# Denominators' reciprocals taken on 128 partitions by way of transfers, and a new order of visits in an attention loop

## The chip, the cores and the metric

The kernel runs on one core of one Trainium2 chip. The metric is the device time of one execution in microseconds (us); the lower the better. Three timed executions of the kernel before took 1839.34, 1840.99 and 1845.72 us, so the median is 1840.99 us.

## The reference

The program computes two residual layers, `x = x + s * g`, each with layer norm. Layer 0 has softmax attention with 16 heads of 64 over 4 batches of 1024 tokens, with 128 features (`s`), and a gated mixture of 8 experts with top-2 routing (`g`). Layer 1 has a linear recurrence and a block-quantised feed-forward. The change touches only the attention of layer 0:

```
q, k, v = split(X @ W_qkv)                      # 16 heads of 64
scores  = q . k / sqrt(64)
weights = softmax(scores)
attn    = weights @ v
s       = attn.reshape(b, s, 16 * 64) @ W_out
```

## The kernel before

`layer0_attention` handles heads two at a time: there are N = 4 batches x 8 = 32 **pairs**. A pair has two halves of 512 queries (`hf` 0 and 1) and in each half 8 key tiles of 128 (KT), so 16 **steps** t. In a step TensorE (PE) makes the scores of 128 keys by 512 queries for two heads (`scores`, six matmuls into `ps_s`), ScalarE (ACT) takes exp into `probs`, GpSimd (POOL) adds the tile to `psum_k` (the sums over keys), and PE multiplies a tile by V (`values`, into `ps_v`). The softmax needs each query's maximum beforehand: PE makes the products again in single precision rounding (`max_products`, into `ps_three`) and VectorE (DVE) reduces them (`row_max`, L1581, or the split forms L1591, L1596, L1603). The maxima of a half are ready in the middle of the half before; `spread` (L1175, L1177) sends them to DRAM and reads them back to 128 partitions (`peak`), and ACT, or DVE for the steps in `BY_V`, writes them negated into `ps_s` before the scores (`seed`).

Two steps make a **visit** (VISITS = 8). Each visit has room for other PE work, the items of the list `VISIT`: the projections of the pair to come (`K0`, `K1`, `Q0`, `Q1`), its V rows (`V0`, `V1`), the denominators (`den1`, `den0`: a matmul of `psum_k` with ones, copied to `den` by ACT, L1453) and the output projection of the pair before (`out0`, `out1`, added to `sT` by DVE, `add_out`, L1641). All of them go through one bank, `ps_x`. That bank is also the last of the three banks of `ps_three`: a visit whose item is not a K or Q projection is **SHARED**, and its second maximum uses banks 1 and 2 (`ps_mx`), so that PE need not wait for DVE to read all of the first maximum. In a visit with a projection both maxima use banks 0 and 1 (`ps_m`), and the second waits until the first is read (`m_done`).

The order of each engine is written out by hand. Before, the visits are K1; Q0 with den1; out0; V0; Q1 with den0; out1; V1; K0: the SHARED visits stand in pairs (out0 and V0, out1 and V1), and of the projections K0, K1 and Q0 follow one another. The reciprocals of the denominators are four DVE instructions of 128x128 a half (`inverse`, L1622), placed between maxima; `normalise` (L1635) multiplies `raw` (the values that ACT took out of `ps_v`) by them; out0 or out1 waits for it.

SyncE (SP) issues all of the direct transfers in one row of instructions. In each pass of its loop, which covers an even and an odd pair, it waits for the last values of the pair before (`v_ready`), then issues `move(1)` (V, 512 KB), `xs_hi` and `xs_lo` (512 KB each), and then the `spread` of each half, with the expert weights' parts between. At the end of the pass it waits for the V1 copy of the odd pair and issues `move(0)`. After the loop, SP waits for that move, and loads the first rows and weights of the next stage.

Of the kernel before, what the change touches and what calls it, by code (L numbers as in the profile page):

```python
# [14 lines left out]
P = 128  # L15
# [967 lines left out]
def layer0_attention(nc, ctx, g):  # L983
# [10 lines left out]
    PARTS = 4  # L994
# [3 lines left out]
    LATE_PRESETS = 5  # L998
# [13 lines left out]
    warm = sb("warm", [P, 1], F32)  # L1012
    x_rows = sb("x_rows", [P, 2, ROW], F32)
# [47 lines left out]
    rden_done = sem("rden_done")  # L1061
# [11 lines left out]
    ones_n_done = sem("ones_n_done")  # L1073
# [5 lines left out]
    VISIT = [("K1",), ("Q0", "den1"), ("out0",), ("V0",), ("Q1", "den0"), ("out1",), ("V1",), ("K0",)]  # L1079
# [4 lines left out]
    BY_V = (3, 13)  # L1084
# [58 lines left out]

    def chunk(name):
        return slice(int(name[1]) * CH, (int(name[1]) + 1) * CH)
# [7 lines left out]
    with nc.Block() as block:  # L1153
        @block.sync
        def _(sp):
# [24 lines left out]
            spread(0, 0)  # L1180
            sp.wait_ge(xa_done, AHEAD["a"])
            move(0)
            with sp.Fori(0, N // 2) as i:
# [6 lines left out]
                spread(n * 2 + 1, 1)  # L1190
                expert_part(n)
                load_part(n + 1)
                spread(n * 2 + 2, 0)
                spread(n * 2 + 3, 1)
                expert_part(n + 1)
                load_part((n + 2) % N)
                spread(n * 2 + 4, 0)
                sp.wait_ge(xa_done, reads(n + 1, "V1"))
                move(0)
            sp.wait_ge(peak_in, (N * 2 + 1) * 16)  # L1200
            sp.wait_ge(we_in, (N + 1) * 16)
# [13 lines left out]
        def _(pe):  # L1215
            def bank_free(n, name):
                names = FIRST if n is None else LAST if n is N else LIST
                at = names.index(name)
                if n is None:
                    if at >= 2:  # L1220
                        pe.wait_ge(READ[READER[names[at - 2]]], reads(n, names[at - 2]))
                elif at:
                    before = names[at - 1]
                    pe.wait_ge(READ[READER[before]], reads(n, before))
                else:
                    pe.wait_ge(xv_done, n * PER["v"] + AHEAD["v"])
# [132 lines left out]
            pe.wait_ge(ones_n_done, 1)  # L1359
# [23 lines left out]
            for n, par in pairs(pe):  # L1383
                for t in range(STEPS):
                    p = t // 2
                    b = (n + (2 if p == VISITS - 1 else 1)) // PAIRS % B
# [41 lines left out]
        def _(act):  # L1428
# [9 lines left out]
            def read(n, name, par):  # L1438
# [12 lines left out]
                else:  # L1451
                    act.wait_ge(rden_done, n * 2 + (2 if name == "den0" else 1))
# [38 lines left out]
            for n, par in pairs(act):  # L1491
                for t in range(STEPS):
# [9 lines left out]
                    if p not in SHARED:  # L1502
                        read(n, VISIT[p][0], par if p == VISITS - 1 else 1 - par)
# [14 lines left out]
                    if p == 5:  # L1518
# [7 lines left out]
        def _(pool):  # L1526
            nc.gpsimd.memset(ones_n[:, :], 1.0).then_inc(ones_n_done, 1)
# [22 lines left out]
            for n, par in pairs(pool):  # L1550
                for t in range(STEPS):
# [14 lines left out]
                    if t != STEPS - 5:  # L1566
# [8 lines left out]
        def _(v):  # L1575
# [55 lines left out]
            def normalise(n, hf):  # L1631
                k = n * 2 + (1 if hf else 2)
                v.wait_ge(rden_done, k + 1)
# [27 lines left out]
            def tiles_of_experts():  # L1661

                v.wait_ge(n_ready, 2)
                v.wait_ge(ones_n_done, 1)
# [48 lines left out]
            v.sem_inc(rden_done, 1)  # L1713
# [27 lines left out]
            for n, par in pairs(v):  # L1741
# [6 lines left out]
                step(0)  # L1748
                step(1)
                low(n, "K1", nxt)  # L1750
                seed(n, 3)
                step(2)
                step(3)
                low(n, "Q0", nxt)
                expert_part(n)
                row_max_upper(n, 4)
                row_max_lower(n, 4)
                inverse(n, 1, 0)
                row_max_shared(n, 5)
                inverse(n, 1, 1)  # L1760
                row_max_upper(n, 6)
                add_out(n, "out0")
                row_max_lower(n, 6)
                row_max_shared(n, 7)
                inverse(n, 1, 2)
                step(8)
                inverse(n, 1, 3)
                step(9)
                low(n, "Q1", nxt)
                normalise(n, 1)  # L1770
                row_max_upper(n, 10)
                row_max_lower(n, 10)
                inverse(n, 0, 0)
                row_max_shared(n, 11)
                seed(n, 13)
                row_max_upper(n, 12)
                add_out(n, "out1")
                row_max_lower(n, 12)
                inverse(n, 0, 1)
                row_max_shared(n, 13)  # L1780
                inverse(n, 0, 2)
                step(14)
                inverse(n, 0, 3)
                step(15)
                low(n, "K0", par)
                normalise(n, 0)
# [675 lines left out]
def program(nc, args, out):  # L2462
# [6 lines left out]
    g.peaks = nc.dram_tensor("peaks", (2, 2 * CH), F32, kind="Internal").ap()  # L2469
    g.results = nc.dram_tensor("results", (2 * NT + ROUTED * CH, D), F32, kind="Internal").ap()  # L2470
# [88 lines left out]
```

## Time and profile before

| What | Value |
|---|---|
| Median of three executions | 1840.99 us |
| The profiled execution's own time | 1841.47 us |
| Its span | 1839.6 us |
| PE busy | 1727.4 us (94%) |
| DVE busy | 1547.9 us (84%) |
| ACT busy | 1459.2 us (79%) |
| POOL busy | 1444.4 us (79%) |
| TensorE's granted clock, mean | 0.98 of full speed |

The span is the time between the first and the last instruction of the profiled execution. Busy times are sums over instructions; a busy PE is not a PE at its peak, since matmuls overlap and their ends are modelled. The attention loop takes from about 75 to 1421 us of the span: 16 passes of two pairs.

### The profile page before, as it was taken

The page shows a single profiled execution, that of the slowest core. Times are in us where ns is not written, and L with a number is a line of the kernel's source. Part 1 is how long each engine was busy: PE and PEld are TensorE (multiplying, and loading weights), DVE is VectorE, ACT ScalarE, POOL GpSimd, SP SyncE. Part 2 cuts the span into 40 slices and gives each one's busy share as a digit, 9 for nine tenths or more (in the row PEclk, how much of TensorE's full clock was granted, in tenths as well). Part 3 has the DMA queues.
Part 4 walks back from the last instruction along what each step waited for, and adds up shares of the span by engine and source line. Part 5 has one row for each costly group of instructions (what it writes and reads, how often), then busy time and mean ns, then how long its engine had stood idle before and what let it go on. Part 6 is the DMA issues. An engine that isn't in the chain of part 4 may idle for free. (4 is left out here: it accounts for less than half of the span.)

```text
span 1839.6 us, 32373 instructions
## 1 busy us (share of the span) xinstructions
PE 1727.4 (94%) x9247; PEld 924.8 (50%) x9247; DVE 1547.9 (84%) x2180; ACT 1459.2 (79%) x1954; POOL 1444.4 (79%) x869
## 2 busy tenths in 40 slices
PE   5899999999999999999999999999999899975687
PEld 5444444444444444444444444444444677763456
DVE  7888888888888888888888888888888878888886
ACT  4488888888888888888888888888888777864553
POOL 5388888888888888888888888888888256654664
PEclk9899999999999999999999999999999999997899
DMA  7212121212212121212122121212122777331000
GB/s 258 79 36 80 36 80 46 80 46 69 78 52 86 34 80 36 80 46 80 46 69 82 51 83 34 80 36 80 46 80 62 241 218 218 115 99 48 0 18 29
DMA packets 125334, 143.31 MB, mean 78 GB/s; under 512 B 26737, under 2 KB 106673, under 8 KB 122098
## 3 DMA queue, kind: packets, MB, share of 16 engines
q1 hardware_dynamic: 120306, 132.61, 23.6%
q0 software_dynamic: 4992, 10.27, 1.7%
q8 instruction: 16, 0.26, 0.1%
q14 instruction: 20, 0.16, 0.0%
HBM read 87.20 MB, written 27.64 MB: 62 GB/s over the span
## 5 line engine op out<-in xcount | busy, mean ns | idle before, releaser
L1562 POOL TENSOR_TENSOR psum_k<-psum_k,probs 128x1024 f32<-128x1024 f32 x384 | 929.3, 2420 | 103.9 <-ACT probs L1499 83.8
L1499 ACT ACTIVATE probs<-ps_s 128x1024 f32<-128x1024 f32 x512 | 497.0, 1024 | 149.9 <-PE ps_s L1319 149.9
L1328 PE MATMUL ps_v<-probs,V 128*64 128x512 f32 x2056 | 497.8, 605 | 0.0
L1581 DVE TENSOR_REDUCE mxh<-ps_three 128x2 f32<-128x1024 f32 x264 | 318.5, 1207 | 98.3 <-PE ps_three L1286 98.2
L1483 ACT ACTIVATE ps_s<-peak 128x1024 f32<-128x1024 f32 x224 | 245.1, 1132 | 0.0
L1483 ACT ACTIVATE ps_s<-qkv_raw 128x1024 f32<-128x1024 f32 x224 | 245.0, 1131 | 0.0
L1622 DVE RECIPROCAL e_y_row<-e_y_row 128x128 f32<-128x128 f32 x256 | 241.0, 941 | 0.0
L1328 PEld LDWEIGHTS ps_v<-probs,V 128*64 128x64 f32 x2056 | 124.8, 136 | 228.6 <-issue 209.7
L1319 PE MATMUL ps_s<-e_ew 64*128 64x512 f32 x1536 | 199.0, 391 | 0.0
L1562 POOL TENSOR_TENSOR psum_k<-probs 128x1024 f32<-128x1024 f32 x64 | 152.8, 2388 | 47.2 <-ACT probs L1499 39.4
L854 POOL DMA_INDIRECT results<-e_y_row,e_y_at x92 | 102.6, 1115 | 82.0 <-ACT e_y_row L795 52.8
L1319 PEld LDWEIGHTS ps_s<-e_ew 64*128 64x128 f32 x1536 | 144.6, 185 | 28.6 <-ACT ps_s L1483 2.7
L1603 DVE TENSOR_REDUCE mxh<-ps_three 128x2 f32<-128x1024 f32 x128 | 150.7, 1178 | 0.1
L1591 DVE TENSOR_REDUCE mxh<-ps_three 128x1 f32<-128x512 f32 x128 | 88.5, 692 | 72.3 <-PE ps_three L1286 70.7
L1286 PE MATMUL ps_three<-e_ew 64*128 64x512 f32 x528 | 131.8, 495 | 6.3 <-DVE mxh L1581 4.9
L1286 PE MATMUL ps_three<-k_hi,q_hi 64*128 64x512 f32 x512 | 126.6, 490 | 0.8
L1286 PEld LDWEIGHTS ps_three<-e_ew 64*128 64x128 f32 x528 | 52.2, 193 | 134.5 <-issue 80.9
L1286 PEld LDWEIGHTS ps_three<-k_hi,q_hi 64*128 64x128 f32 x512 | 50.2, 191 | 125.0 <-issue 79.5
L1319 PE MATMUL ps_s<-q_hi,k_hi 64*128 64x512 f32 x512 | 101.3, 391 | 0.0
L1319 PE MATMUL ps_s<-q_lo,k_hi 64*128 64x512 f32 x512 | 101.2, 390 | 0.0
L1319 PE MATMUL ps_s<-q_hi,k_lo 64*128 64x512 f32 x512 | 100.9, 389 | 0.0
L779 ACT ACTIVATE e_relu<-e_ps_z 128x512 f32<-128x512 f32 x124 | 74.6, 602 | 33.0 <-PE e_ps_z L708 30.0
(320 smaller groups left out, 3184.4 us busy)
## 6 DMA issues: line engine op xcount, KB each, us to landing
e_ew<-w_split SPq DMA_DIRECT2D x23, 1024.0 KB
qkv_raw<-peaks SPq DMA_DIRECT2D x33, 512.0 KB, 3.9
V<-e_x_raw SPq DMA_DIRECT2D x33, 512.0 KB, 3.6
peak<-peaks SPq DMA_DIRECT2D x32, 512.0 KB, 4.3
xs_hi<-xh SPq DMA_DIRECT2D x16, 512.0 KB, 4.0
xs_lo<-xl SPq DMA_DIRECT2D x16, 512.0 KB, 5.0
rows<-in_blank_d SPq DMA_DIRECT2D x4, 1483.5 KB, 16.9
e_x_raw<-rows SPq DMA_DIRECT2D x23, 258.0 KB
```

Source lines behind the costliest of these rows:

```text
L779: nc.scalar.activation(r[:, q % NZ, :], ps_z[q % NZ][:, :], ACT.Relu).then_inc(relu_done, 1)
L854: nc.gpsimd.indirect_dma_start(g.results[:, :], bass.IndirectOffsetOnAxis(ap=y_at[s][:, t, 0:1], axis=0), y_row[s][:, t, :], None).then_in ...
L1286: ins = nc.tensor.matmul(m[:, x, :], q[rows, :], k_hi[par][rows, kh * CH:(kh + 1) * CH], start=True, stop=True)
L1319: ins = nc.tensor.matmul(o[:, x, :], lhs[par][rows, keys], rhs[par][rows, qs], start=False, stop=True, skip_group_check=True)
L1328: ins = nc.tensor.matmul(ps_v[rows, :], V[par][:, kt, rows], probs[:, t % RING, x, :], start=kt == 0, stop=kt == KT - 1)
L1483: nc.scalar.activation(ps_s[t % 2][:, :, :], peak[hf][:, :, :].rearrange("p c x -> p x c"), ACT.Copy, scale=-1.0).then_inc(seeded, 1)
L1499: nc.scalar.activation(probs[:, t % RING, :, :], ps_s[t % 2][:, :, :], ACT.Exp, scale=SCALE).then_inc(p_done, 1)
L1562: nc.gpsimd.tensor_tensor(acc, probs[:, (t - 1) % RING, :, :] if kt == 1 else acc, probs[:, t % RING, :, :], ALU.add).then_inc(add_done, 1)
L1581: nc.vector.tensor_reduce(mxh[:, kh, t, :], max_bank(unit, i)[:, :, :], AX.X, ALU.max).then_inc(m_done, 1)
L1591: nc.vector.tensor_reduce(mxh[:, kh, q, 1:2], ps_m[:, 1, :], AX.X, ALU.max).then_inc(m_upper, 1)
L1603: nc.vector.tensor_reduce(mxh[:, kh, q, :], ps_mx[:, :, :], AX.X, ALU.max).then_inc(m_done, 1)
L1622: ins = nc.vector.reciprocal(rden[:, cols], den[:, cols])
```

## The change

The four reciprocals of 128x128 per half become one of 128x8. The denominators of a head are the same on its 64 partitions, so one row of 512 of each head is sent to 64 partitions of 8 words (`flatten`, two SBUF to SBUF transfers), DVE inverts it, the result goes to DRAM (`inverse_out`) and is read back to 64 partitions of 512 words for each head (`inverse_back`, two transfers). `spread` is split in two, and `half_pair` sets the order of SP's issues in each half. The ACT copy of the denominators no longer waits for the reciprocals of the half before.

The visits become Q0 with den1; out0; K1; V0; Q1 with den0; out1; K0; V1: each projection is followed by a SHARED visit. DVE's order follows, in a function `half` that is the same for both halves; the DVE seeds are those of steps 3 and 11, not 3 and 13. ACT's weight staging (`stage`) and POOL's `w_lo` move forward with K0. Outside the loop, `ones_n_done` becomes part of `preset`.

```
-    BY_V = (3, 13)
+    BY_V = (3, 11)
-    VISIT = [("K1",), ("Q0", "den1"), ("out0",), ("V0",), ("Q1", "den0"), ("out1",), ("V1",), ("K0",)]
+    VISIT = [("Q0", "den1"), ("out0",), ("K1",), ("V0",), ("Q1", "den0"), ("out1",), ("K0",), ("V1",)]
...
+            def spread_back(unit, hf):
+
                 sp.wait_ge(mx_out, unit * 16 + 16)
                 sp.dma_start(peak[hf][:, :, :].rearrange("p c x -> p (c x)"), g.peaks[hf:hf + 1, :].to_broadcast([P, 2 * CH])).then_inc(peak_in, 16)
 
+            def flatten(n, hf):
+
+                sp.wait_ge(xa_done, reads(n, f"den{hf}"))
+                for x in range(2):
+                    sp.dma_start(flat_den[x * DH:(x + 1) * DH, :], den[x * DH:x * DH + 1, :].rearrange("a (c k) -> a c k", c=DH)).then_inc(inv_moved, 16)
+
+            def inverse_out(k):
+
+                sp.wait_ge(inv_done, k + 1)
+                sp.dma_start(g.shares[:, :].rearrange("a (c k) -> (a c) k", c=DH), flat_inv[:, :]).then_inc(inv_moved, 16)
+
+            def inverse_back(k):
+
+                sp.wait_ge(inv_moved, inv_moved_out(k))
+                for x in range(2):
+                    sp.dma_start(rden[x * DH:(x + 1) * DH, :], g.shares[x:x + 1, :].to_broadcast([DH, CH])).then_inc(inv_moved, 16)
+
+            def half_pair(n, unit, hf):
+
+                k = n * 2 + 1 - hf
+                flatten(n, hf)
+                inverse_out(k)
+                spread(unit, hf)
+                inverse_back(k)
+                spread_back(unit, hf)
...
-                spread(n * 2 + 1, 1)
+                half_pair(n, n * 2 + 1, 1)
...
-                    act.wait_ge(rden_done, n * 2 + (2 if name == "den0" else 1))
...
-            def inverse(n, hf, part):
-
-                cols = slice(part * P, (part + 1) * P)
-                v.wait_ge(xa_done, reads(n, f"den{hf}"))
-                ins = nc.vector.reciprocal(rden[:, cols], den[:, cols])
-                if part == PARTS - 1:
-                    ins.then_inc(rden_done, 1)
+            def inverse(n, hf):
+
+                v.wait_ge(inv_moved, flat_moved(n * 2 + 1 - hf))
+                nc.vector.reciprocal(flat_inv[:, :], flat_den[:, :]).then_inc(inv_done, 1)
...
+                def half(hf, late, early, par):
+
+                    t = KT - KT * hf
+                    step(t)
+                    step(t + 1)
+                    low(n, early, nxt)
+                    seed(n, t + 3)
+                    row_max_upper(n, t + 2)
+                    row_max_lower(n, t + 2)
+                    row_max_shared(n, t + 3)
+                    inverse(n, hf)
+                    add_out(n, f"out{1 - hf}")
+                    step(t + 4)
+                    step(t + 5)
+                    low(n, late, par)
+                    if hf:
+                        expert_part(n)
+                    row_max_upper(n, t + 6)
+                    row_max_lower(n, t + 6)
+                    row_max_shared(n, t + 7)
+                    normalise(n, hf)
```

DVE before, from the second seed to the third visit of an even pair (`e_y_row` is `den` on the right and `rden` on the left of the arrow; `ps_three` in L1591 is the first maximum of a SHARED visit; L1641 is `add_out`):

```order
L1739 TENSOR_SCALAR ps_s<-qkv_raw 128x1024 [waits peak_in]
...
L1591 TENSOR_REDUCE mxh<-ps_three 128x1 [waits mx_done,m_ready]
L1596 TENSOR_REDUCE mxh<-ps_three 128x1
L1621 REGISTER_ALU
L1622 RECIPROCAL e_y_row<-e_y_row 128x128 [waits xa_done]
L1602 REGISTER_ALU
L1603 TENSOR_REDUCE mxh<-ps_three 128x2 [waits m_ready]
L1622 RECIPROCAL e_y_row<-e_y_row 128x128 [waits xa_done]
L1588 REGISTER_ALU
L1591 TENSOR_REDUCE mxh<-ps_three 128x1 [waits m_ready]
L1639 ISA
L1641 ISA [waits x_ready]
L1641 TENSOR_TENSOR sT<-ps_three,sT 128x512
```

DVE now, at the end of the second visit and the start of the third (L1662 is `inverse`, L1679 is `add_out`, L1622 is now the whole row maximum):

```order
L1644 TENSOR_REDUCE mxh<-ps_three 128x2 [waits m_ready]
L1651 REGISTER_ALU [waits m_done]
L1652 TENSOR_REDUCE mx<-mxh 128x8 [waits mx_out]
L1661 ISA
L1662 RECIPROCAL flat_inv<-flat_den 128x8 [waits inv_moved]
L1677 ISA
L1679 ISA [waits x_ready]
L1679 TENSOR_TENSOR sT<-ps_three,sT 128x512
L1619 ISA
L1622 TENSOR_REDUCE mxh<-ps_three 128x2 [waits mx_done,m_ready]
```

One reciprocal stands where four were spread out, it waits for a transfer and not for ACT, and `add_out` and the maximum of the third visit stand behind it.

SP before, at the head of its loop's pass:

```order
L1159 DMA V<-e_x_raw 128x8x128 [waits v_ready]
L1188 ISA
L1188 DMA xs_hi<-xh 128x1024
L1189 REGISTER_ALU
L1189 DMA xs_lo<-xl 128x1024
L1174 REGISTER_ALU
L1175 DMA peaks<-mx 128x2x4 [waits mx_done]
L1176 ISA
L1177 DMA peak<-peaks 128x1024 [waits mx_out]
```

SP now, from the same place (L1197 is `flatten`, L1202 `inverse_out`, L1208 `inverse_back`; `e_y_row` is `den` in the first and `rden` in the last):

```order
L1230 DMA xs_lo<-xl 128x1024
L1195 ISA
L1197 DMA flat_den<-e_y_row 64x1x8 [waits xa_done]
L1197 DMA flat_den<-e_y_row 64x1x8
L1202 DMA shares<-flat_inv 128x8 [waits inv_done]
L1185 REGISTER_ALU
L1186 DMA peaks<-mx 128x2x4 [waits mx_done]
L1206 ISA
L1208 DMA e_y_row<-shares 64x512 [waits inv_moved]
L1208 DMA e_y_row<-shares 64x512
L1190 ISA
L1191 DMA peak<-peaks 128x1024 [waits mx_out]
```

The transfers of `flatten` stand right behind the three large ones, and the maxima's way to DRAM and back stands behind the reciprocals'.

## Rows read from the trace of the kernel before

**Rows 1.** Stage windows, the attention loop: busy us by engine, clock, DMA share.

```profile
120.00:1440.00 1320.00, 1306.35 (x7215) 619.40 (x7212) 1119.26 (x1281) 1134.20 (x1340) 1156.98 (x623) 1.00 0.21 65
```

**Rows 2.** The page's groups: busy us, mean ns, idle before.

```profile
L1622 DVE RECIPROCAL e_y_row<-e_y_row 128x128 f32<-128x128 f32 x256 | 241.0, 941 | 0.0
```

**Rows 3.** Timeline of PE, four visits of an odd pair: start, duration, line.

```profile
716.68 0.50 PE L1286 MATMUL ps_three<-e_ew 64*128 64x512 f32 x2
717.02 0.40 PE L1319 MATMUL ps_s<-q_hi,k_hi 64*128 64x512 f32 x2
...
718.73 1.94 PE L1328 MATMUL ps_v<-probs,V 128*64 128x512 f32 x8
...
721.51 0.51 PE L1286 MATMUL ps_three<-e_ew 64*128 64x512 f32 x2
...
723.84 1.94 PE L1328 MATMUL ps_v<-probs,V 128*64 128x512 f32 x8
725.71 0.39 PE L1255 MATMUL ps_three<-wv_hi,xs_hi 128*128 x1
...
726.61 0.51 PE L1286 MATMUL ps_three<-e_ew 64*128 64x512 f32 x2
...
728.43 0.50 PE L1286 MATMUL ps_three<-e_ew 64*128 64x512 f32 x2
...
729.76 1.94 PE L1328 MATMUL ps_v<-probs,V 128*64 128x512 f32 x8
...
732.49 0.50 PE L1286 MATMUL ps_three<-e_ew 64*128 64x512 f32 x2
```

**Rows 4.** Timeline of DVE, the same pair.

```profile
722.67 0.68 DVE L1641 TENSOR_TENSOR sT<-ps_three,sT 128x512 f32 x1
723.27 0.68 DVE L1596 TENSOR_REDUCE mxh<-ps_three 128x1 f32<-128x512 f32 x1
...
727.15 1.23 DVE L1581 TENSOR_REDUCE mxh<-ps_three 128x2 f32<-128x1024 f32 x1 [1.12 <-PE ps_three L1286]
```

**Rows 5.** Timeline of SP's issues, an even pair.

```profile
584.55 0.61 SPq L1159 DMA_DIRECT2D V<-e_x_raw  x1
...
588.41 0.38 SPq L1175 DMA_DIRECT2D peaks<-mx  x1
591.29 0.33 SPq L1177 DMA_DIRECT2D peak<-peaks  x1
```

**Rows 6.** Windows, the end of that pair's large transfers.

```profile
590.50:591.00 0.50, 0.50 (x6) 0.41 (x8) 0.07 (x1) 0.50 (x1) 0.50 (x1) 1.00 0.32 17
```

**Rows 7.** SP's issues, the next even pair.

```profile
672.61 0.38 SPq L1175 DMA_DIRECT2D peaks<-mx  x1
676.63 0.33 SPq L1177 DMA_DIRECT2D peak<-peaks  x1
```

**Rows 8.** PE, first visit of the even pair of rows 5.

```profile
579.32 0.50 PE L1286 MATMUL ps_three<-e_ew 64*128 64x512 f32 x2
...
582.58 1.94 PE L1328 MATMUL ps_v<-probs,V 128*64 128x512 f32 x8
```

**Rows 9.** POOL in that visit.

```profile
582.27 0.39 POOL L1538 COPY x_rows<-x_tok 128x256 f32 x1
```

**Rows 10.** The page's transfers: count, KB each, us to landing.

```profile
peak<-peaks SPq DMA_DIRECT2D x32, 512.0 KB, 4.3
...
peaks<-mx SPq DMA_DIRECT2D x65, 4.0 KB, 2.5
```

**Rows 11.** SP's issues at the end of the attention stage.

```profile
1416.98 0.65 SPq L1159 DMA_DIRECT2D V<-e_x_raw  x1
...
1423.85 0.36 SPq L376 DMA_DIRECT2D e_ew<-w_split  x1
1430.41 0.33 SPq L637 DMA_DIRECT2D dt<-in_dt_d  x1
```

**Rows 12.** ACT's last instruction of the stage.

```profile
1425.83 0.60 ACT L1453 ACTIVATE e_y_row<-ps_three 128x512 f32<-128x512 f32 x1 [0.26 <-PE ps_three L1266]
```

More of the change, by code:

```diff
@@ L993, in layer0_attention @@
     EARLY = 4
-    PARTS = 4
     ADDS = KT - 1
@@ L997, in layer0_attention @@
     PRESETS = 3
-    LATE_PRESETS = 5
+    ONES_PRESETS = 4
+    LATE_PRESETS = 6
     HEADS = [slice(x * DH, (x + 1) * DH) for x in range(2)]
@@ L1012, in layer0_attention @@
     warm = sb("warm", [P, 1], F32)
+    flat_den = sb("flat_den", [P, 2 * CH // P], F32)
+    flat_inv = sb("flat_inv", [P, 2 * CH // P], F32)
     x_rows = sb("x_rows", [P, 2, ROW], F32)
@@ L1060, in layer0_attention @@
     xv_done = sem("xv_done")
-    rden_done = sem("rden_done")
+    inv_done = sem("inv_done")
+    inv_moved = sem("inv_moved")
     picked = sem("picked")
@@ L1142, in upper, with flat_moved, inv_moved_out, inv_moved_back @@
         return n * len(SHARED) + SHARED.index(t // 2) + 1
+    def flat_moved(k):
+        return k * 80 + 32
+    def inv_moved_out(k):
+        return k * 80 + 48
+    def inv_moved_back(k):
+        return k * 80 + 80
     def chunk(name):
@@ L1200, in _ @@
             sp.wait_ge(peak_in, (N * 2 + 1) * 16)
+            sp.wait_ge(inv_moved, inv_moved_back(N * 2 - 1))
             sp.wait_ge(we_in, (N + 1) * 16)
@@ L1225, in bank_free @@
                 else:
-                    pe.wait_ge(xv_done, n * PER["v"] + AHEAD["v"])
+                    pe.wait_ge(xa_done, n * PER["a"] + AHEAD["a"])
             def projection(n, name, b):
@@ L1358, in _ @@
             pe.wait_ge(picks_done, 1)
-            pe.wait_ge(ones_n_done, 1)
+            pe.wait_ge(preset, ONES_PRESETS)
             for k, left in enumerate((g.before, ones_n)):
@@ L1385, in _ @@
                     p = t // 2
-                    b = (n + (2 if p == VISITS - 1 else 1)) // PAIRS % B
+                    b = (n + (2 if VISIT[p][0] == "K0" else 1)) // PAIRS % B
                     unit, i = maximum(t)
@@ L1502, in _ @@
                     if p not in SHARED:
-                        read(n, VISIT[p][0], par if p == VISITS - 1 else 1 - par)
+                        read(n, VISIT[p][0], par if VISIT[p][0] == "K0" else 1 - par)
                     for k in (t + 1, t + 2):
@@ L1517, in _ @@
                         read(n, name, 1 - par)
-                    if p == 5:
+                    if p == VISITS // 2:
                         stage(n)
@@ L1565, in _ @@
                         scatter(hf)
-                    if t != STEPS - 5:
+                    if t != STEPS - 7:
                         continue
@@ L1632, in normalise @@
                 k = n * 2 + (1 if hf else 2)
-                v.wait_ge(rden_done, k + 1)
+                v.wait_ge(inv_moved, inv_moved_back(k - 1))
                 v.wait_ge(raw_done, k)
@@ L1746, in step @@
                     row_max(n * 2 + unit, i)
[L1748 to L1786, printed above, removed]
+                def half(hf, late, early, par):
[18 more added lines that the diff above has]
+                    normalise(n, hf)
+                half(1, "K1", "Q0", nxt)
+                half(0, "K0", "Q1", par)
             add_out(N, "out0")
@@ L2469, in program @@
     g.peaks = nc.dram_tensor("peaks", (2, 2 * CH), F32, kind="Internal").ap()
+    g.shares = nc.dram_tensor("shares", (2, CH), F32, kind="Internal").ap()
     g.results = nc.dram_tensor("results", (2 * NT + ROUTED * CH, D), F32, kind="Internal").ap()
```

13 lines of the change are left out of this document (6 added, 7 removed).

## The prediction

> **What bounds the kernel now.** I first read the windows of the attention loop: PE is busy 1306 of 1320 us, DVE 1119, ACT 1134, POOL 1157, at full clock [rows 1]. So the loop is paced by PE, and every us that it stands still counts once. Busy PE time hides short stalls, since the ends of matmuls are modelled; so I then read PE's timeline by the distance from one start to the next, visit by visit.
>
> A SHARED visit that never waits is the one with out0: 716.68 to 721.51, 4.83 us, of which 2.05 lie before the values [rows 3]. In a visit with a projection, the second maximum waits until DVE has read the first: 726.61 to 728.43, 1.82 us, where DVE's reduction starts 0.54 us after PE's maximum and was idle before, so that it was not itself late [rows 3, 4]. The visit with V0 (721.51 to 726.61, 5.10 us) is SHARED too, yet takes 2.33 us to its values and not 2.05: its second maximum needs the shared bank, which DVE is still reading for out0 (`add_out`, 722.67 to 723.35) [rows 3, 4]. One pass of the loop, two pairs, takes 672.61 - 588.41 = 84.20 us [rows 5, 7].
>
> **The visits in their new order.** The pieces, from [rows 3]:
> - values before a fast item 725.71 - 723.84 = 1.87; V rows 726.61 - 725.71 = 0.90; second maximum and projection before the values 729.76 - 728.43 = 1.33; values and denominators 732.49 - 729.76 = 2.73; values and output projection 721.51 - 718.73 = 2.78.
> - Q with den: 1.82 + 1.33 + 2.73 = 5.88.
> - out, SHARED: 2.05 + 2.78 = 4.83.
> - K: 1.82 + 1.33 + 1.87 = 5.02. But `add_out` now stands before the first maximum on DVE. PE goes on 0.34 us after it starts a maximum (716.68 to 717.02), so a result is there 0.54 - 0.34 = 0.20 after the start of what follows it; I take the same for out. And `add_out` holds DVE for 723.27 - 722.67 = 0.60, so the reduction starts at 0.83 and not 0.54: + 0.29, and 5.31.
> - V, SHARED behind a projection and no longer behind out: 2.05 + 1.87 + 0.90 = 4.82.
>
> A half is 5.88 + 4.83 + 5.31 + 4.82 = 20.84, a pass four of them, 83.36, against 84.20. Sixteen passes give **-13.4 us**. The visits themselves can hardly miss by more than 0.1 us a half, so -20 to -7.
>
> **The reciprocals.** 256 instructions of 0.94 us leave DVE and 64 short ones come [rows 2]. DVE does not pace the loop, so the 241 us are worth only the waits already removed above: none besides. The new one has 8 columns for 128: at least 0.06 us in proportion, at most 0.94; I take 0.2, near the lower end.
>
> **The new wait on DVE.** `inverse` waits for `flatten`, and behind it on DVE stand `add_out` and the first maximum of the K1 or K0 visit, whose end PE's second maximum waits for. What covers the wait is that `add_out` can't start before out is there: 5.88 + 4.83 + 0.20 = 10.91 us after the start of the half.
>
> In three of a pass's four halves that is enough. The denominators are ready on PE at 5.88 + 0.20, ACT's copy takes 0.60 [rows 12], so it ends by about 6.8, the two transfers, at some 0.4 each, are issued by 7.6, and a small transfer lands 2.5 us after its issue by the median, 4.0 at the longest that I use [rows 10, 7], counted from the issue's start (7.2 for the second): 9.7, and at the longest 11.2. I take nothing for it.
>
> In the first half of an even pair, SP has just issued V, xs_hi and xs_lo, 1.5 MB. Before, V goes out at 584.55, 5.23 after the visit's start; the values start at 3.26 there and at 1.82 + 1.33 = 3.15 now, so V goes out at 5.12 [rows 5, 8]. `flatten` follows behind xs_lo's issue. What a small transfer meets there is seen on `peaks<-mx`: issued at 588.41 it was back only at 591.29, just after the DMA engines had run dry (share 0.32 in 590.5 to 591.0) [rows 5, 6]. That is 6.74 after V's issue, whatever its own issue time. So `flat_den` is there at 5.12 + 6.74 = 11.86, the reciprocal and hand-over end at 12.1, and `add_out` starts 1.2 us late. PE's second maximum of the K1 visit is late by the same 1.2, and nothing gives it back. Sixteen times: **+19.2 us**. The next pass's small transfer took 4.02 and not 2.88 [rows 5, 7]; with 1.14 more each time it would be +37, and if a write that stays in SBUF is confirmed 0.4 sooner, +13. I take 19.2, by the nearer row; both of these transfers end in DRAM, `flatten` does not, so the longer is the less likely.
>
> The Trainium skill (DMA: Bandwidth & Descriptors, Queues, rings and completion order) says that a transfer from SP is laid on one ring per DMA engine and that each engine takes descriptors in ring order, which speaks against this place for `flatten`; the trace agrees, by the 591.29 just named. The same page (Anatomy of one DMA) gives a transfer a fixed cost of about 2.0 us besides its bytes; taken alone that would put `flat_den` at 9.9, before 10.91, and the loop at -13.4 us; the 2.88 and 4.02 us of these rows do not bear it out in an even pair.
>
> **Other moved work.** den1 moves a visit forward, to 5 us after the pair's start; POOL has ended the sums by 582.27, 2.95 after it [rows 8, 9]: no wait. The ways back: in the even half the reciprocals go out at 12.2, the maxima's write behind them, the read of `peak` at 15 to 16, landing 4.3 later and after `rden`'s 256 KB: 20 to 21 [rows 10]. ACT wants it for seed 8 some 3 us into the V0 visit, at 10.91 - 0.20 + 5.31 + 1.2 + 3.2 = 20.4: just hidden, worth at most 0.5 us each time (8 us). `normalise` in the V0 visit comes later than `rden`. The seed moved from step 13 to 11 changes hands between engines that both have room.
>
> **The end of the stage.** V1 is now in the last visit. Its copy ended at 1416.98, some 0.8 us into the last visit (0.20 and the copy's 0.60), and SP's last issue at 1424.21, 7.23 later, while ACT ended at 1426.43, 9.45 later, and all engines went on at 1430.41 [rows 11, 12]. Now the copy can't end before 4.82 + 0.6, so SP ends at 12.7 or later, ACT at 10.2. If the next stage starts 4 us after the last arrival, +2.5; if the 4 us already hid it, 0; if it waits for the large loads, which all start 5 us later, +5. I take **+2.5**.
>
> **Sum.** -13.4 + 19.2 + 2.5 = +8.3 on the profiled execution's 1841.47, so 1849.8; that execution is 0.5 above the median of 1840.99, so 1849.3. I say 1850.
>
> **Rivals.**
> - *`flat_den` is in time* (small transfers slip past the large ones, or SBUF writes are confirmed at once): the even pairs' wait goes, -13.4 + 2.5, 1830. For it: the 1.2 us hang on an order at the DMA engines seen on one kind of transfer. Against: that transfer was held in both even pairs shown.
> - *The waits cancel*: 0.6 to 0.8 us late, or the visits gain 0.3 more: 1843. For it: the margin is the difference of two numbers near 11.
> - *The late transfer is slow* (4.02 rather than 2.88 throughout), and `peak` comes late behind it: +18 to +26 on the forecast, 1868 to 1875; in half of the passes, 1860. It decides once the landing is past 12.5.
> - *The new order gains nothing by itself*: `add_out` in front of a maximum costs what its bank cost before; -13.4 becomes -3, and with the wait it is 1860.
>
> **Chances.** The forecast's mechanism, 1846.5 to 1857: 0.39. In time, 1830: 0.26. Cancel, 1843: 0.22. The last two, 1858 and above: 0.13. A change of 0.3% is 5.5 us, about what a measurement here can tell. Faster by more 0.26, within 0.22, slower by more 0.52 (0.39 and 0.13). The range 1830 to 1862 leaves out the end of each side; the forecast's own is 1846 to 1857.
>
> **What would show it.** SHARED visits of 4.8 us on PE in a row with projections of 5.3 and 5.9; `flat_den`'s second transfer in even pairs landing with the end of xs_lo, DVE idle before `inverse` there for about 1 us and, in odd pairs, not; passes of 84.6 us (83.4 if the first rival holds). A wait of DVE in all four halves, or an ACT wait at seed 8, would make me wrong on the slow side; a landing before 11 us in even pairs on the fast side.

## The result, and the profile after

The changed kernel takes 1860.31 us (median of 6 runs, 1854.81 to 1865.87), the kernel before beside it 1840.16 us (6 runs): a ratio of 1.0109, 95% interval 1.0084 to 1.0134. It is slower, by 20 us where 9 were forecast. The profiled executions differ by 18.44 us (1859.91 and 1841.47).

The windows of the attention loop, as in [rows 1] (us, then busy us of PE, PEld, DVE, ACT and POOL, clock, DMA share, GB/s):

```profile
120.00:1440.00 1320.00, 1281.74 (x7186) 618.14 (x7183) 974.77 (x1085) 1125.33 (x1333) 1160.17 (x620) 1.00 0.25 74
```

DVE works 145 us less than in [rows 1], and PE is busy 25 us less in the same stretch: it stands still more often. (The stretch of before takes in the change of stage at 1430, which now comes at 1450. And DVE's gain is smaller than its 241 us of reciprocals: `normalise`, for one, whose operands both lie in SBUF, takes 2.12 us by the mean where it took 1.52.) The new reciprocal, by its line (duration in ns, then what DVE was idle for):

```profile
L1662 DVE RECIPROCAL flat_inv<-flat_den x64: 202/203/205, 86.7 to 1429.2; 128x8 f32<-128x8 f32 x64
its engine sat idle before it (us, times) until:
  DMA flat_den<-e_y_row: 40.9, 16
```

64 of 0.20 us stand for the 256 of 0.94 [rows 2], and DVE waits for the transfer 16 times, once in each pass, 2.6 us each by the mean. SP's issues in an even pair, to be held against [rows 5]:

```profile
594.12 0.52 SPq L1229 DMA_DIRECT2D xs_hi<-xh  x1
594.76 1.07 SPq L1230 DMA_DIRECT2D xs_lo<-xl  x1
595.97 2.56 SPq L1197 DMA_DIRECT2D flat_den<-e_y_row  x2
600.44 0.32 SPq L1202 DMA_DIRECT2D shares<-flat_inv  x1
```

DVE behind it:

```profile
600.21 0.20 DVE L1662 RECIPROCAL flat_inv<-flat_den 128x8 f32<-128x8 f32 x1 [2.53 <-DMA flat_den<-e_y_row]
600.54 0.69 DVE L1679 TENSOR_TENSOR sT<-ps_three,sT 128x512 f32 x1
601.15 1.22 DVE L1622 TENSOR_REDUCE mxh<-ps_three 128x2 f32<-128x1024 f32 x1
```

And PE in that half, which began at 588.09, against the visits of [rows 3]:

```profile
597.80 1.03 PE L1319 MATMUL ps_three<-e_y_row,wo 128*64 128x512 f32 x4
598.76 0.51 PE L1328 MATMUL ps_three<-k_hi,q_hi 64*128 64x512 f32 x2
...
602.42 0.50 PE L1328 MATMUL ps_three<-k_hi,q_hi 64*128 64x512 f32 x2 [1.78 <-DVE mxh L1622]
...
605.62 0.51 PE L1328 MATMUL ps_three<-k_hi,q_hi 64*128 64x512 f32 x2
```

The output projection of out0 is issued by 598.76; DVE begins `add_out` only at 600.54, since the reciprocal ahead of it in its queue waits for `flat_den`. The first maximum follows, and PE's second stands 1.78 us. The K1 visit lasts 605.62 - 598.76 = 6.86 us. Not all of DVE's 2.53 us is loss, since `add_out` has to wait for out0 in any case: it starts 1.78 us after the start of the visit here, and 0.35 us after it in the run "no transfers" below, so the wait makes it 1.43 us late. In the second half of the same pair there is no wait:

```profile
621.18 0.51 PE L1328 MATMUL ps_three<-k_hi,q_hi 64*128 64x512 f32 x2
623.29 0.51 PE L1328 MATMUL ps_three<-k_hi,q_hi 64*128 64x512 f32 x2 [0.21 <-DVE mxh L1622]
...
626.57 0.50 PE L1328 MATMUL ps_three<-k_hi,q_hi 64*128 64x512 f32 x2
```

K0 there takes 5.39 us. Read the passes by the distance from one issue of `xs_hi` to the next (15 distances): before all lie between 84.17 and 84.28; after, twelve lie between 85.06 and 85.13, and the first, fifth and thirteenth are 87.23, 86.57 and 86.64. All together are 18.5 us longer, which is the whole difference of the profiled executions.

The first pass has a longer wait than the others, 3.17 us on DVE and 2.43 on PE, so 0.7 of its extra 2.1 us is that wait:

```profile
86.66 0.20 DVE L1662 RECIPROCAL flat_inv<-flat_den 128x8 f32<-128x8 f32 x1 [3.17 <-DMA flat_den<-e_y_row]
```

```profile
88.88 0.50 PE L1328 MATMUL ps_three<-k_hi,q_hi 64*128 64x512 f32 x2 [2.43 <-DVE mxh L1622]
```

The rest of it, and all of what is extra in the fifth and the thirteenth, comes with a fall of the clock.

In the fifth pass, PE (first fence) and the windows (second):

```profile
430.73 0.61 PE L1328 MATMUL ps_three<-k_hi,q_hi 64*128 64x512 f32 x2 [1.78 <-DVE mxh L1622]
431.27 0.79 PE L1280 MATMUL ps_three<-xh,w_hi 128*128 x1
...
432.84 2.69 PE L1370 MATMUL ps_v<-probs,V 128*64 128x512 f32 x8
```

```profile
430.00:432.00 2.00, 1.27 (x4) 0.83 (x5) 1.30 (x2) 0.33 (x1) 2.00 (x1) 0.75 0.21 53
432.00:434.00 2.00, 2.00 (x7) 0.72 (x7) 1.02 (x2) 1.05 (x2) 1.92 (x2) 0.50 0.96 281
434.00:436.00 2.00, 2.00 (x10) 0.63 (x8) 0.82 (x2) 1.57 (x2) 0.54 (x1) 0.90 0.17 61
```

Right behind the stall of 1.78 us the granted clock is 0.50, the 1.2 GHz level, and the values take 2.69 us where [rows 3] have 1.94. The same is seen in the first and the thirteenth pass and in no other. The loop of before never leaves the 2.4 GHz level.

At the end of the stage the copy of V1 is later, as foreseen, but the rest is not (SP's issues; compare [rows 11]):

```profile
1441.55 0.67 SPq L1170 DMA_DIRECT2D V<-e_x_raw  x1
...
1450.13 0.36 SPq L637 DMA_DIRECT2D dt<-in_dt_d  x1
```

From V's issue to the next stage's first load it was 13.43 us and is now 8.58. What SP waited for last there, in the kernel before and in the changed one (us, times, longest):

```profile
SPq L1153 <- PEq L1153: 6.0, 1, 6.0
```

```profile
SPq L1164 <- PEq L1164: 0.2, 1, 0.2
```

Before, SP was ready 6.0 us ahead of PE's sequencer; now it is ready 0.2 us ahead.

### The profile page after: what moved, and what is told of

Read it like the earlier page. It is cut to its first block and busy times, and to the rows that moved or that the text cites. A ratio compares the mean times of both kernels' runs of the same rounds, so it can differ in the third digit from the quotient of the medians.

```text
span 1858.1 us, 32755 instructions
## 1 busy us (share of the span) xinstructions
PE 1713.7 (92%) x9247; PEld 931.7 (50%) x9247; DVE 1405.6 (76%) x1988; ACT 1455.0 (78%) x1954; POOL 1452.3 (78%) x869
## 5 line engine op out<-in xcount | busy, mean ns | idle before, releaser
L1603 POOL TENSOR_TENSOR psum_k<-psum_k,probs 128x1024 f32<-128x1024 f32 x384 | 939.4, 2446 | 125.6 <-ACT probs L1540 105.5
L1622 DVE TENSOR_REDUCE mxh<-ps_three 128x2 f32<-128x1024 f32 x264 | 322.7, 1222 | 79.8 <-PE ps_three L1328 79.5
L1644 DVE TENSOR_REDUCE mxh<-ps_three 128x2 f32<-128x1024 f32 x128 | 156.8, 1225 | 39.8 <-PE ps_three L1328 38.7
L1632 DVE TENSOR_REDUCE mxh<-ps_three 128x1 f32<-128x512 f32 x128 | 88.4, 691 | 91.7 <-PE ps_three L1328 91.7
L1673 DVE TENSOR_TENSOR e_y_row<-e_y_row 128x512 f32<-128x512 f32 x64 | 135.5, 2117 | 0.0
```

Of the source, the lines that this page charges most:

```text
L1603: nc.gpsimd.tensor_tensor(acc, probs[:, (t - 1) % RING, :, :] if kt == 1 else acc, probs[:, t % RING, :, :], ALU.add).then_inc(add_done, 1)
L1622: nc.vector.tensor_reduce(mxh[:, kh, t, :], max_bank(unit, i)[:, :, :], AX.X, ALU.max).then_inc(m_done, 1)
L1632: nc.vector.tensor_reduce(mxh[:, kh, q, 1:2], ps_m[:, 1, :], AX.X, ALU.max).then_inc(m_upper, 1)
L1644: nc.vector.tensor_reduce(mxh[:, kh, q, :], ps_mx[:, :, :], AX.X, ALU.max).then_inc(m_done, 1)
L1673: nc.vector.tensor_tensor(attn[:, :], raw[:, :], rden[:, :], ALU.mult).then_inc(attn_done, 1)
```

## The experiments

Each is the changed kernel with the edit shown, unless said otherwise. "Passes" are the 15 distances between issues of `xs_hi`. A ratio is to times of the kernel before taken beside the run; "one time" stands for a single timed execution, of which only the trace is used.

| Run | Ratio to before (95%) | Passes, us |
|---|---|---|
| kernel before | 1 | 84.2 |
| changed kernel | 1.0109 (1.0084 to 1.0134) | 85.1; three of 86.6 to 87.2 |
| flatten first | 1.0018 (1.0007 to 1.0030) | 83.7 to 85.0 |
| no transfers | 0.9963 (0.9949 to 0.9977) | 83.6 |
| transfers only | 1.0002 (0.9991 to 1.0012) | 84.1 |
| short xs_lo | one time | four of 83.8 to 83.9; ten of 85.1; first 85.7 |
| xs early | 0.9971 (0.9956 to 0.9986) | 83.6 |
| split last | one time | six of 88.8 to 88.9; eight of 92.0 to 92.3; first 93.6 |
| wait alone | 1.0102 (1.0078 to 1.0125) | 85.1; two of 86.5 |
| changed kernel again | 1.0122 (1.0095 to 1.0148) | 85.1; four of 86.5 to 88.4 |
| no split | one time | 83.8 to 84.0; first 87.3 |
| wait doubled | one time | 86.1; 87.8 to 89.1 in eleven |

**Flatten first.** SP issues `flat_den` ahead of the bulk.

```
+                flatten(n, 1)
                 move(1)
...
-                half_pair(n, n * 2 + 1, 1)
+                inverse_out(n * 2)
+                spread(n * 2 + 1, 1)
+                inverse_back(n * 2)
+                spread_back(n * 2 + 1, 1)
```

> The changed kernel, with one move in SP's row: in the first half of an even pair the two small transfers of the denominators are issued before V, xs_hi and xs_lo and not behind them. Theory A (the loss is the wait behind these 1.5 MB): DVE no longer idles before the reciprocal (2.53 us in each of 16 passes in the changed kernel), PE's 1.78 us stall in the K1 visit goes, a pass takes 83.6 us (four halves of 20.9) for 85.1, no fall of the granted clock inside the loop, and the ratio to the kernel before is 0.994 to 0.996. Rival B (the new order or the traffic of the added transfers costs by itself): passes stay at 85, ratio 1.008 or more. A half-way result would come from the reciprocals' way back, which now stands behind the large transfers.

DVE's wait for `flat_den` is gone in all passes but the first, the clock stays at the 2.4 GHz level through the loop, and most of the loss is gone with it; the ratio of 0.994 to 0.996 that theory A expects isn't reached. What is left is the way back: `peak` now stands behind the bulk, and ACT waits for it at seed 8, once in each pass and 18.9 us in all.

```profile
584.62 1.16 SPq L1197 DMA_DIRECT2D flat_den<-e_y_row  x2
...
587.37 1.05 SPq L1231 DMA_DIRECT2D xs_lo<-xl  x1
...
593.56 0.50 SPq L1191 DMA_DIRECT2D peak<-peaks  x1
```

```profile
598.64 2.11 ACT L1528 ACTIVATE ps_s<-peak 128x1024 f32<-128x1024 f32 x2 [1.29 <-DMA peak<-peaks]
```

**No transfers.** The new order of visits; DVE takes one quarter of the reciprocals directly, and the other three quarters are left out.

```
-                v.wait_ge(inv_moved, flat_moved(n * 2 + 1 - hf))
-                nc.vector.reciprocal(flat_inv[:, :], flat_den[:, :]).then_inc(inv_done, 1)
+                v.wait_ge(xa_done, reads(n, f"den{hf}"))
+                nc.vector.reciprocal(rden[:, 0:P], den[:, 0:P]).then_inc(inv_done, 1)
```

> The new order of visits with none of the added transfers; DVE inverts one quarter of the denominators (128 columns of 512) straight from ACT's copy, and the other three quarters are left out (they are one). It is the new order by itself, with DVE nearly as free as in the changed kernel. Theory A: 83.6 us a pass, ratio 0.994 to 0.996, the same as with the small transfers issued first. Rival B1 (the order costs): 84.5 or more a pass, ratio above 1.003. Rival B2 (the order is fine and the added transfers cost, by traffic at the DMA engines): this run is at 0.995 and the one with the transfers issued first is not.

The order, with DVE's reciprocals gone, is worth 0.6 us a pass: 83.6 against 84.2. The next run puts the share of DVE in it at 0.1 or less. The rival by which the order gains nothing falls.

**Transfers only.** The kernel before with its own order of visits, its reciprocals taken by `flatten`, `inverse_out` and `inverse_back`, `inverse` placed one visit behind the copy of the denominators. In a pair's first half SP issues the maxima's write ahead of `flatten`.

```
-                inverse(n, 1, 0)
...
-                inverse(n, 1, 1)
+                inverse(n, 1)
...
-                inverse(n, 1, 2)
...
-                inverse(n, 1, 3)
```

> The order of visits before, with the reciprocals by transfers and no longer in four parts on DVE; the small reciprocal is placed where den1 or den0 was copied one visit earlier, so that nothing large is in the way of its transfers. Theory A: freeing DVE gives back the wait of PE before V1 (0.17 to 0.24 us and one weight load a pair, seen only there) and nothing else, 83.4 to 84.0 a pass, ratio 0.995 to 1.000; the added transfers cost nothing. Rival B2 (the added transfers cost by themselves): slower than before, 1.005 or more.

84.1 us a pass. The added transfers and the reciprocals that leave DVE are together worth 0.1 us: where hardly anything waits for `flat_den` (DVE does so 29 times, 4.7 us in all), the transfers cost nothing that can be seen.

**Short xs_lo.** The transfer of `xs_lo` in the loop is cut to 8 columns.

```
-                sp.dma_start(xs_lo[:, :].bitcast(F32), g.xl[:, batch].bitcast(F32)).then_inc(xs_in, 16)
+                sp.dma_start(xs_lo[:, 0:8].bitcast(F32), g.xl[:, bass.ds((n + 2) // PAIRS % B * T, 8)].bitcast(F32)).then_inc(xs_in, 16)
```

> The changed kernel with the transfer of xs_lo in the loop cut from 1024 columns to 8 (the rest of xs_lo keeps the first batch's values): 1.0 MB in front of the denominators' transfers for 1.5. Theory A: they land when what is in front has drained, 512 KB at about 400 GB/s or 1.3 us earlier, so DVE's idle time before the reciprocal falls from 2.5 to about 1.2 us and PE's stall from 1.8 to 0.4 or 0.5; a pass 83.9 us. If instead the landing were set by a fixed latency, the idle time would stay at 2.5.

Only four passes did what was expected. The reciprocal now starts 4.88 us after the issue of `xs_hi` in a short pass and 5.12 in a long one, against 6.09 in the changed kernel: with 0.5 MB less ahead of it `flat_den` is 1.0 to 1.2 us earlier, so it does stand behind the bulk. But 0.24 us between these two passes became 1.2. Over all passes but the first, DVE waits 1.32 or 1.33 us for `flat_den` in the short ones and 1.34 to 1.56 in the long ones: the step is a sharp one. DVE in a short pass, and from 591.50 on in a long one:

```profile
507.40 0.20 DVE L1664 RECIPROCAL flat_inv<-flat_den 128x8 f32<-128x8 f32 x1 [1.33 <-DMA flat_den<-e_y_row]
...
512.29 0.42 DVE L1669 TENSOR_TENSOR we_lo<-we_raw,we_hi 128x256 fp32r<-128x256 f32 x1
513.37 0.69 DVE L1634 TENSOR_REDUCE mxh<-ps_three 128x1 f32<-128x512 f32 x1 [0.66 <-PE ps_three L1330]
...
591.50 0.20 DVE L1664 RECIPROCAL flat_inv<-flat_den 128x8 f32<-128x8 f32 x1 [1.56 <-DMA flat_den<-e_y_row]
...
596.39 2.44 DVE L1669 TENSOR_TENSOR we_lo<-we_raw,we_hi 128x256 fp32r<-128x256 f32 x1
598.75 0.68 DVE L1634 TENSOR_REDUCE mxh<-ps_three 128x1 f32<-128x512 f32 x1
```

The same instruction of 256 columns takes 0.42 us and 2.44. POOL and PE in the long pass:

```profile
596.15 2.40 POOL L1605 TENSOR_TENSOR psum_k<-psum_k,probs 128x1024 f32<-128x1024 f32 x1
```

```profile
599.56 0.51 PE L1330 MATMUL ps_three<-k_hi,q_hi 64*128 64x512 f32 x2 [0.76 <-DVE mxh L1634]
```

A POOL add began at 596.15, 0.24 us ahead of DVE's instruction, and ended at 598.55; DVE's ended at 598.83. The maximum behind it was late, and PE's next. In the short pass DVE came at a border between two adds, and the add that began with it took 0.3 us longer:

```profile
512.29 2.69 POOL L1605 TENSOR_TENSOR psum_k<-psum_k,probs 128x1024 f32<-128x1024 f32 x1
```

That gave a new theory, tested by "split last" and "no split".

**Xs early.** Both bulk loads go out at the end of the pass, behind `move(0)`, and `flatten` stands ahead of `move(1)`; `xs(m)` issues the two loads for pair m.

```
             with sp.Fori(0, N // 2) as i:
...
+                flatten(n, 1)
                 move(1)
-                sp.dma_start(xs_hi[:, :].bitcast(F32), g.xh[:, batch].bitcast(F32)).then_inc(xs_in, 16)
-                sp.dma_start(xs_lo[:, :].bitcast(F32), g.xl[:, batch].bitcast(F32)).then_inc(xs_in, 16)
-                half_pair(n, n * 2 + 1, 1)
+                inverse_out(n * 2)
+                spread(n * 2 + 1, 1)
+                inverse_back(n * 2)
+                spread_back(n * 2 + 1, 1)
...
                 move(0)
+                xs(n + 4)
```

> The changed kernel with SyncE's queue put in another order: the two bulk loads xs_hi and xs_lo are issued straight behind move(0), at the end of the pass, and flatten stands ahead of move(1). In the run with flatten first, flat_den was in time but the way back (peak and rden) stood behind the bulk, and passes went 83.7 to 85.0. Theory A (the loss of the change is the wait behind the bulk, nothing else): with neither way behind a freshly issued bulk the passes come to what the order gives without transfers, 83.6 to 83.8 us against 84.2 before, so ratio 0.994 to 0.998 and no stretch of the loop at the 1.2 GHz level. Rival: the bulk still moves in the same stretch, only from earlier, and V's transfer now shares the engines with it; then the small transfers or V land late and passes stay at 84.3 to 85.1, ratio 1.001 to 1.010.

This version is faster than both kernels: 1835.07 us (12 runs) beside 1838.96 (17 runs). Passes are 83.6, as without transfers, and the K1 visit of an even pair is 5.43 us:

```profile
578.89 0.55 SPq L1222 DMA_DIRECT2D xs_hi<-xh  x1
579.55 1.05 SPq L1223 DMA_DIRECT2D xs_lo<-xl  x1
583.62 1.15 SPq L1197 DMA_DIRECT2D flat_den<-e_y_row  x2
```

```profile
587.66 0.51 PE L1338 MATMUL ps_three<-k_hi,q_hi 64*128 64x512 f32 x2
589.88 0.51 PE L1338 MATMUL ps_three<-k_hi,q_hi 64*128 64x512 f32 x2 [0.35 <-DVE mxh L1632]
593.09 0.51 PE L1338 MATMUL ps_three<-k_hi,q_hi 64*128 64x512 f32 x2
```

The passes alone would give 16 x 0.58 = 9 us, and the medians show 4. One place of the rest can be read: from the start of the last values to the next stage's first load it is 10.47 us here (1415.24 to 1425.71), 7.64 in the changed kernel (1442.49 to 1450.13) and 7.39 in the kernel before (1423.02 to 1430.41). The last pass still loads 1 MB that nobody reads, now right ahead of the next stage's loads, and SP waits 2.5 us for its `xs_lo` there. Around that change of stage the granted clock also stays at the 1.2 GHz level for longer than in the kernel before (it is 0.50 from 1422 to 1434 here, and there from 1431 to 1437). A version without that load was not tried.

**Split last.** The short xs_lo again, with DVE's split of the expert weights behind the normalising.

```
-                    if hf:
-                        expert_part(n)
                     row_max_upper(n, t + 6)
                     row_max_lower(n, t + 6)
                     row_max_shared(n, t + 7)
                     normalise(n, hf)
+                    if hf:
+                        expert_part(n)
```

> The run with xs_lo's transfer in the loop cut to 8 columns (xs_lo is loaded once ahead of the loop, so later batches are computed with the first batch's low halves), with VectorE's split of the expert weights (we_lo) moved from behind k_lo to behind the normalising. In that run passes were of two kinds, 83.85 and 85.1 us; in a long one the reciprocal started 0.24 us later, and we_lo, which came to start 0.24 us behind the start of a GpSimd add instead of at its border, took 2.44 us instead of 0.42. Theory: it is VectorE's two-input instruction held until the GpSimd add ends that makes 1.2 us of a delay of 0.24. Then with the split out of the way all passes are within 0.3 us of 83.9 and there are no 85.1 ones. Rival: the longer passes come from the maxima or from peak landing late, and the long we_lo only lies in a wait that is there anyway; then both kinds of pass stay, 83.85 and 85.1, wherever the split stands.

Neither came: passes are 88.8 to 92.3 us (1949.99 in all). The new place was a bad choice, for the split is now held every time, PE stands 2.4 us behind it in every pair, and the clock falls twice in each of the passes of 92 us and not in those of 88.8:

```profile
L1669 DVE TENSOR_TENSOR we_lo<-we_raw,we_hi x32: 2590/2597/2604, 97.7 to 1504.2; 128x256 fp32r<-128x256 f32 x32
```

The instruction starts 0.4 us behind the start of a POOL add here (97.67 and 97.28) and ends 0.28 behind its end. It shows that the length goes by the place and not by the work, but it can't tell whether the split made the two kinds of pass.

**No split.** The short xs_lo, the split left out.

```
-                nc.vector.tensor_tensor(we_lo[:, :], we[:, :], we_hi[:, :].bitcast(F32), ALU.subtract).then_inc(we_lo_done, 1)
+                nc.vector.memset(idle[:, :], 1.0).then_inc(we_lo_done, 1)
```

> The kernel with the short xs_lo transfer again (xs_lo is loaded once ahead of the loop, so later batches are computed with the first batch's low halves), and VectorE's split of the expert weights left out: a memset of 8 columns stands in its place, and the rounded halves are stored where the low halves belong. In the run with the split behind the normalising it took 2.60 us in every pair, right behind the start of a GpSimd add, so that run could not tell. Theory (the split held behind a GpSimd add made 1.2 us of a delay of 0.24): without it all passes stay within 0.3 us of 83.9, none is at 85.1. Rival (the long split lay in a wait that is there anyway): passes of both kinds, 83.85 and 85.1, as before.

Fourteen passes lie between 83.79 and 84.03, none at 85.1 (the first, 87.3, has a wait of 3.1 us on DVE and a fall of the clock). DVE still waits 1.3 to 1.5 us for `flat_den` in the others, and against 83.6 it costs 0.2 to 0.4, most of it being time in which out0 isn't there yet. So the long passes of "short xs_lo" were the split held behind POOL's add.

**Wait alone.** "No transfers" with 296 more columns of reciprocal ahead of `add_out`, in the first half of the even pair only.

```
+                    if hf and par == 1:
+                        nc.vector.reciprocal(rden[:, P:P + 296], den[:, P:P + 296])
                     add_out(n, f"out{1 - hf}")
```

> The new order of the visits without any of the added transfers (one quarter of the reciprocals directly on VectorE, the other three left out, as in the run without transfers, whose passes are 83.6 us), and in the first half of the even pair alone 296 more columns of reciprocal ahead of add_out: at 0.94 us for 128 columns some 2.1 us, of which 0.5 fall into a wait, so add_out some 1.6 us late, as in the changed kernel (12.45 against 10.91). Theory A (the wait alone is the loss, one for one): passes of 85.1 to 85.3, ratio 1.004 to 1.008 with 1.5 x 15 = +23 us over the run without transfers; if the falls of the granted clock come from TensorE's stall, one to four passes show a stretch at the 1.2 GHz level and are 1.5 us longer. Rival B (the loss is contention by the transfers, or the clock falls need them): passes stay below 84.2 and the clock stays at the 2.4 GHz level through the loop.

Passes of 85.1, with none of the added transfers, and two at the lower clock. The ratio came out at 1.0102, above the 1.004 to 1.008 expected, and beside the 1.0122 that the changed kernel showed on the same chip. That the passes agree to the hundredth is partly chance: the K1 visit is 6.60 us here and 6.86 in the changed kernel, and the V0 visit behind it 5.14 and 4.88, since the split is held for 1.72 us here and 1.46 there. The wait costs 1.2 of the 1.5 us directly and 0.3 by way of the split. The pass of the first fall (PE, then windows):

```profile
512.23 0.51 PE L1323 MATMUL ps_three<-k_hi,q_hi 64*128 64x512 f32 x2 [1.50 <-DVE mxh L1618]
513.56 3.63 PE L1365 MATMUL ps_v<-probs,V 128*64 128x512 f32 x8
```

```profile
514.00:516.00 2.00, 2.00 (x6) 0.49 (x4) 1.70 (x2) 2.00 (x3) 2.00 (x1) 0.50 0.00 0
```

The values take 3.63 us instead of 1.94, at a DMA share of 0: none of the added transfers is needed for the fall.

**Changed kernel again.** No edit.

> The changed kernel once more, to see which of its numbers return. Ratio 1.008 to 1.014; ordinary passes 85.1 us. If the stretches at the 1.2 GHz level belong to the program they are in the same passes as before (the first, the fifth and the thirteenth); if they depend on when TensorE's stall falls, they are in other passes or in another number of them, and the time of a run moves by 1.5 us for each.

The ordinary passes return (85.03 to 85.10); the longer ones are the first, second, seventh and thirteenth. Which of the later passes are hit is not a property of the program, and 1.5 us for each is part of the spread between its executions. In the first pass PE stands 3.46 us, before the clock falls there too.

**Wait doubled.** "Wait alone" with 384 + 128 columns.

```
-                        nc.vector.reciprocal(rden[:, P:P + 296], den[:, P:P + 296])
+                        nc.vector.reciprocal(rden[:, P:P + 384], den[:, P:P + 384])
+                        nc.vector.reciprocal(idle[:, :], den[:, P:P + P])
```

> As the run with the wait alone (new order, no added transfers, one quarter of the reciprocals done, three left out), but 512 columns of reciprocal ahead of add_out in the first half of the even pair instead of 296: 384 at about 2.5 us and 128 at 0.94. TensorE's stall at the second maximum of the K1 visit then grows by some 1.5 us, from 1.8 to 3.3. If the wait costs one for one, an ordinary pass is 86.6 us (85.1 + 1.5). If the fall of the granted clock comes from the length of TensorE's stall, it is in many more passes than the 2 of 15 of that run, at 1.5 us each (pass 88.1); if it has another cause (when the stall falls, and nothing else), it stays in 1 to 3 passes.

Four ordinary passes are at 86.1 (86.6 expected), and eleven of 15 are at 87.8 to 89.1. PE's stall grew by 1.4 us and an ordinary pass by 1.0, since the split, which now comes later, is no longer held (0.41 to 0.44 us in all 32 pairs) and gives 0.3 back. The stall and the clock behind it:

```profile
529.22 0.79 PE L1324 MATMUL ps_three<-k_hi,q_hi 64*128 64x512 f32 x2 [2.88 <-DVE mxh L1619]
```

```profile
528.00:530.00 2.00, 0.78 (x3) 0.34 (x3) 1.17 (x2) 0.00 (x0) 1.92 (x2) 0.59 0.44 158
530.00:532.00 2.00, 2.00 (x7) 1.07 (x7) 1.23 (x1) 0.37 (x1) 1.93 (x1) 0.50 0.00 0
532.00:534.00 2.00, 2.00 (x6) 0.48 (x4) 1.02 (x2) 2.00 (x3) 0.00 (x0) 0.50 0.00 0
```

A longer stall makes the fall frequent, and in eight of twelve falls it also lasts longer than in "wait alone".

## Why the prediction was right and wrong

The direction was right, and so was the mechanism: one wait in a pass, in the place that was named. The size was not: +9 us were forecast and +20 came. That 1860 lies inside the range of 1830 to 1862 is luck, for its upper end was put there for other causes (a transfer as slow as that of [rows 7] in every pass, ACT waiting for `peak`, an order that gains nothing), none of which came; the forecast's own range ended at 1857, and 1858 and above had a chance of 0.13. Two terms of the sum were mis-sized, both to the fast side, and a third, the clock, was put at nothing without a reason.

The step that failed is "PE's second maximum of the K1 visit is late by the same 1.2, and nothing gives it back. Sixteen times: +19.2 us". The wait measured 1.48 us a pass, 23.7 us, and behind it PE also ran at half speed in three passes, 4.4 us more. With it failed the order's -13.4 us, which measured -9.3. By steps:

- *The order of the visits*, forecast 83.36 a pass: right in kind, 0.25 too small. Without transfers, and in "xs early", passes are 83.6. The pieces as measured: Q with den 5.89 (5.88), out 4.78 (4.83), K 5.36 to 5.44 (5.31), V 4.84 to 4.88 (4.82). The gain is 0.58 a pass and not 0.84: over 16, 9.3 us instead of 13.4. K was the worst: `add_out` was taken to start 0.20 us into its visit and starts at 0.35 there ("no transfers"). (The sum of that piece also has a slip: 0.20 and 0.60 make 0.80, not 0.83, so K by its own terms was 5.28, and the miss a little larger.)
- *The wait for `flat_den`*, forecast 1.2 us in the even pairs' first half and none in the other three: right in place and count (16 waits). It costs 85.10 - 83.62 = 1.48, so 23.7 us instead of 19.2. `add_out` was to start 12.1 after the start of the half and started at 12.45 (600.54 - 588.09), the reciprocal at 12.12 where the landing was put at 11.86. The size was taken from the nearer of two rows of another transfer, 6.74 us after V's issue and 7.89 [rows 5, 7]; it was 6.98. "Wait alone" shows that a wait is enough for the loss, "transfers only" that the transfers cost nothing by themselves, and "xs early" that the loss goes when only the place of the bulk loads changes.
- *What the forecast lacked*: with a stall that long the clock can fall. Three passes were 2.1, 1.5 and 1.5 us longer, 5.1 us; 0.7 of it is the first pass's longer wait, which the forecast lacked too, and 4.4 the clock. Why the first pass waits longer stays open.
- *The end of the stage*, forecast +2.5: not there. The last values start 7.39 us before the next stage's first load in the kernel before (1423.02 to 1430.41) and 7.64 after. Of the three cases that the prediction named, the second came, "if the 4 us already hid it, 0": SP, which had 6.0 us to spare, used them up. The rows, of before and of after, PE:

```profile
1423.02 1.92 PE L1328 MATMUL ps_v<-probs,V 128*64 128x512 f32 x8
```

```profile
1442.49 1.89 PE L1370 MATMUL ps_v<-probs,V 128*64 128x512 f32 x8
```

- *`peak` just hidden*: it was, in the changed kernel, where ACT nowhere waits for it in the loop; it is what remains once `flatten` goes first.
- *DVE's 241 us worth nothing by themselves*: right, 0.1 us a pass ("transfers only").

Together, over 16 passes: -9.3 + 23.7 + 5.1 + 0.25 = +19.8, against 18.4 in the profiled execution. (The 15 distances give 15 x 0.90 + 5.1 = 18.6.)

## What to carry to other kernels

Freeing an engine that isn't the bound is worth nothing; what its new input waits for, and what is queued behind that wait, is the price. Issue a small transfer that an in-order engine waits for ahead of bulk loads, and its way back too, or move the bulk to a stretch where nobody waits: here that turned 1.01 into 0.997. Where a TensorE stall comes to 1.5 us or more, count also what the lower clock may take behind it.

## What the runs showed of the hardware

- *The clock can fall with a single stall of PE, and does so more often the longer the stall.* At 1.5 us it fell with 2 of 16 stalls ("wait alone"), at 1.7 to 1.8 with 2 of 15 and 3 of 15 (the changed kernel twice), at 2.2 to 2.5 with 20 of 33 ("split last"), at 2.9 with 12 of 16 ("wait doubled"); in the first passes, at 2.4 to 3.5, in three runs of four. With the six stalls of 0.9 to 1.0 in "short xs_lo" it never fell, nor in the loop of the kernel before. A fall cost 1.4 to 1.5 us behind stalls of 1.5 to 1.8, and 1.6 to 2.8 with those of 2.9. Why one stall of 1.78 us is followed by it and the next equal one isn't, stays open.
- *A DVE instruction with two operands in SBUF is held until a POOL add that began ahead of it ends*: 0.42 us at a border, 1.5 in the changed kernel, 2.44 to 2.67 close behind the start of an add of 2.4 to 2.7 us. In the three passes read it ended 0.28 us behind the add each time. The reductions beside it, which read PSUM, stay at 0.69 and 1.23 us. The Trainium skill (SBUF — State Buffer, Who interferes with whom) says that such an instruction contends with a GpSimd instruction that reads SBUF; the trace agrees. So a delay of 0.24 us can cost 1.2, when it shifts an instruction across such a border; in "short xs_lo" a delay of 0.01 did (a wait of 1.34 instead of 1.33 us, and a split of 2.67).
- *A small transfer behind bulk loads of the same queue comes late.* The two transfers of `flat_den` land 1.8 us after their issue by the median of all halves, and issuing the two takes 1.16 us at 1426.32, where no bulk is ahead of them. Behind the bulk the issues from 595.97 on take 2.56 us, and DVE has `flat_den` only at 600.21, 4.2 us after the first; with 0.5 MB less ahead of them it has it 1.0 to 1.2 us sooner.
